# An attention block on one Trainium2 core: one wide transpose and eight small transfers for the softmax maxima

## The chip, the cores and the metric

The kernel is one program on one core of a Trainium2 chip. The metric is the device time of one execution in microseconds (us), the median over the runs.

## What is computed

The input is x (8 batches, 512 tokens, 128 features). Per batch the reference does, in float32:

```python
h = layernorm(x) * (1 + ca) + sa
x = x + ga * attention(h)        # 16 heads of 8 features, rotary, causal, softmax, projection
h = layernorm(x) * (1 + cb) + sb
x = x + gb * spikes(relu(h @ W_fc.T)**2 @ W_proj.T)   # counts of 5 threshold steps / 5
```

What matters for this change is the softmax: the weights are exp(scale * (q.k - m)) over the allowed keys, divided by their sum, and m is the row maximum of the scores of one query and one head.

## The kernel before, in words

**Halves.** The work goes in 16 halves, two per batch; a half is 8 of the 16 heads of one batch. The scores are computed twice. The first time the queries lie on the partitions (`scores_for_max`, L442, into `s_bank`, 21 units a half) and VectorE (DVE) reduces each block to a negated maximum (`maxima`, L771, the reduction at L783, into `negmax`, 128 x 8 x 4: queries of 64 for two heads on the partitions, eight blocks `i` of 64 queries, four pairs of heads `p`). The second time the keys lie on the partitions (`scores_for_exp`, L477, into `t_bank`, 18 units `u` or slots a half), ScalarE (ACT) takes the exponential of a whole unit (L669), and TensorE multiplies it by the values (`probs_times_v`, L505, into `o_bank`).

**How the maximum gets into the second product.** q and k are stored as rows of `qf` and `kf` (72 rows: three bfloat16 parts of q, k for 8 features). Two more rows, `FR:KX`, hold in `qf` the negated maximum in two bfloat16 parts (high and remainder), and ones in `kf`, so that the second product comes out with the maximum already subtracted. Those rows need the maxima laid out as rows along the queries, and `negmax` has them as columns. The way from one to the other, once per half, is:

- GpSimd (POOL) splits `negmax` into two bfloat16 parts `mparts` (`split_maxima`, L1028 and L1030);
- TensorE turns them (`transpose_maxima`, L464): eight transposes of 128 x 8 into `m_bank`, which is the bank `a_bank` read as bfloat16; it gives 8 rows of 1024;
- ACT copies the 8 x 1024 block to `mrow` (`maxima_out`, L675);
- SP sends `mrow` with one transfer to the two rows of `qf` (`place_maxima`, L356) and the semaphore `maxrow` counts its landing;
- the first `scores_for_exp` of the half waits for `maxrow` (L480).

I call the point where TensorE goes from the last slot of half n-1 to the first slot of half n **boundary n** (boundary 0 is the first slot of all).

**What sets the order.** Every engine has its instruction list written out by hand; there is no planner. TensorE's list per slot is: maxima scores up to `scores_ahead(u)` (31 units in advance), then the exp scores of the slot, then products with the values, then, in given slots, the transposes of the maxima (slot `M_AT` = 14 of 18), projections of a later batch (`A_AT`), and projection and feed-forward of an earlier one (`D_AT`, `Y_AT`). ACT copies the maxima just ahead of the exponential of slot 15. The list of TensorE is strictly in order at the level of waits: while the first slot of a half waits for `maxrow`, nothing behind it starts.

**SP's queue.** All transfers go through SP, in a written order (L402 to L425). After `place_maxima(n)` come stores of q and k parts (L333), and `spread` (L345, L351), which loads `qf` and `kf` for the half after next and waits until the exp scores of the half before are all done; then `move_outputs` with four transfers of `den` and four of `o_t` (L362, L366), and `spread_reciprocals`. A `den` transfer goes from 2 partitions of 512 float32 to 16 partitions of 64.

Of the kernel before, what the change touches and what calls it, by code (L numbers as in the profile page):

```python
# [7 lines left out]
BF16 = mybir.dt.bfloat16  # L8
ALU = mybir.AluOpType
# [3 lines left out]
P = 128  # L13
NB, SEQ, D = 8, 512, 128
# [4 lines left out]
FR = NPART * NPART * HD  # L19
MR = 2  # L20
KX = FR + MR
# [7 lines left out]
C = 64  # L29
NC = SEQ // C  # L30
HALVES = 2 * NB
HP = 4
HH = 2 * HP
NP = H // 2
RING = 3
# [76 lines left out]
def reach(eng, sem, count):  # L112

    if count > 0:
        eng.wait_ge(sem, count)


def adaln_kernel(nc, x, wqk, bqk, wv, bv, wo, bo, wfc, wpr, ct, wmod, cosn, sinn, place, out):
# [9 lines left out]
    with ExitStack() as ctx:  # L128
        def sb(name, shape, dt=F32):
            return ctx.enter_context(nc.sbuf_tensor(name, shape, dt))  # L130
# [4 lines left out]
        def sem(name):  # L135
            return ctx.enter_context(nc.semaphore(name))
# [15 lines left out]
        identb = sb("identb", [P, P], BF16)  # L152
# [29 lines left out]
        qf = sb("qf", [P, RING, HH, SEQ], BF16)  # L182
        kf = sb("kf", [P, RING, HH, SEQ], BF16)
        negmax = sb("negmax", [P, 2, NC, HP])
        mparts = sb("mparts", [P, NC, MR, HP], BF16)
        mrow = sb("mrow", [MR * HP, 2 * SEQ], BF16)
        probs = sb("probs", [P, NU, SEQ])
        o_raw = sb("o_raw", [P, 2, SEQ])
        o_t = sb("o_t", [P, SEQ])
# [24 lines left out]
        m_bank = a_bank[:, :].bitcast(BF16)  # L214
# [40 lines left out]
        maxrow = [sem("maxrow0"), sem("maxrow1")]  # L255
        s_ready = sem("s_ready")
        s_free = sem("s_free")
        mhigh_done = sem("mhigh_done")
        mparts_done = sem("mparts_done")
        m_ready = sem("m_ready")  # L260
        m_free = sem("m_free")
# [46 lines left out]
        def _(sp):  # L308
# [43 lines left out]

            def place_maxima(n):
                sp.wait_ge(m_free, n + 1)
                dst = qf[FR:KX, n % RING].rearrange("r (p a) c -> r p (a c)", a=2)
                sp.dma_start(dst, mrow[:, :]).then_inc(maxrow[n % 2], 16)  # L356

            def move_outputs(b, half):
                sp.wait_ge(o_free, 2 * b + half + 1)
# [36 lines left out]
            for j in range(NPART):  # L396
                store_part(1, 0, j)
            place_maxima(0)
            for j in range(NPART - 1):
                store_part(1, 1, j)  # L400

            for b in range(NB):  # L402
                if b + 1 < NB:
                    store_part(b + 1, 1, 2)
                    spread(2 * b + 2)
                if b > 0:
                    move_outputs(b - 1, 1)
                    spread_reciprocals(b - 1, 1)
                if b + 3 < NB:
                    load_x(b + 3)  # L410
                place_maxima(2 * b + 1)
                if b + 1 < NB:
                    spread(2 * b + 3)
                if b > 1:
                    store_out(b - 2)
                move_outputs(b, 0)
                spread_reciprocals(b, 0)
                if b + 2 < NB:
                    for j in range(NPART):
                        store_part(b + 2, 0, j)  # L420
                    store_part(b + 2, 1, 0)
                if b + 1 < NB:
                    place_maxima(2 * b + 2)
                if b + 2 < NB:
                    store_part(b + 2, 1, 1)  # L425
# [8 lines left out]
        def _(pe):  # L434
            def by_halves(bank, cols, weights, data, start=True, stop=True):

                for a in range(2):
                    own = slice(C * a, C * (a + 1))
                    last = nc.tensor.matmul(bank[own, cols], weights[:, own], data, start=start, stop=stop)  # L439
                return last  # L440
# [23 lines left out]
            def transpose_maxima(n):  # L464
                pe.wait_ge(mparts_done, n + 1)
                reach(pe, m_free, n)

                if n % 2 == 0:
                    pe.wait_ge(a_free, 3 * min(n // 2 + 2, NB))
                else:  # L470
                    pe.wait_ge(v_placed, 2 * min((n - 1) // 2 + 2, NB))
                for i in range(NC):
                    to = m_bank[0:MR * HP, :].rearrange("m (a q) -> m a q", a=2)[:, :, C * i:C * (i + 1)]
                    last = nc.tensor.transpose(to, mparts[:, i].rearrange("p r h -> p (r h)"), identb[:, :])
                last.then_inc(m_ready, 1)

            def scores_for_exp(u):  # L477
                n, v = divmod(u, NU)
                if v == 0:
                    pe.wait_ge(maxrow[n % 2], 16 * (n // 2 + 1))  # L480
                reach(pe, e_done, u - 1)
                bank, slot = t_bank[u % 2], n % RING
                blocks = T_BANKS[v]
                for at, (p, kb, col) in enumerate(blocks):
                    w = SEQ - C * kb
                    for a in range(2):
                        nc.tensor.matmul(bank[C * a:C * (a + 1), col:col + w],  # L487
                                         kf[0:KX, slot, 2 * p + a, C * kb:C * (kb + 1)],
                                         qf[0:KX, slot, 2 * p + a, C * kb:SEQ], start=at == 0, stop=False)
                for at, (p, kb, col) in enumerate(blocks):  # L490
                    for a in range(2):
                        last = nc.tensor.matmul(bank[C * a:C * (a + 1), col:col + C], identb[:, C * a:C * (a + 1)],  # L492
                                                causal_t[:, C * a:C * (a + 1)], start=False, stop=at == len(blocks) - 1)
                last.then_inc(t_ready, 1)
# [106 lines left out]
            for k in range(NS, NS + 3):  # L601
                scores_for_max(k)
            transpose_maxima(0)
            for k in range(NS + 3, scores_ahead(-1)):
                scores_for_max(k)
            pe.wait_ge(ones_placed, 16)

            for u in range(SLOTS):
                n, v = divmod(u, NU)
                b, at = divmod(u, PER_BATCH)  # L610
                for k in range(scores_ahead(u - 1), scores_ahead(u)):
                    scores_for_max(k)
                scores_for_exp(u)
                for kb in PV_AFTER.get(v, ()):
                    probs_times_v(n, kb)
                if n > 0:
                    for kb in PV_LATE.get(v, ()):
                        probs_times_v(n - 1, kb)
                if v == M_AT and n + 1 < HALVES:
                    transpose_maxima(n + 1)  # L620
                if at in A_AT and b + 1 < NB:
                    a_task(b + 1, A_AT[at])
                if at - PER_BATCH in A_AT and b + 2 < NB:
                    a_task(b + 2, A_AT[at - PER_BATCH])
                steps, products = (D_LAST, Y_LAST) if b == final else (D_AT, {})
                if at in steps and b > 0:
                    d_task(b - 1, steps[at])
                if at in products:
                    d_task(b - 1, Y_, range(products[at], products[at] + 1))
                if at + PER_BATCH in Y_AT and b > 1:  # L630
                    d_task(b - 2, Y_, range(Y_AT[at + PER_BATCH], Y_AT[at + PER_BATCH] + 1))
# [15 lines left out]
            for t, cols in enumerate(tokens):  # L647
                pe.wait_ge(last_on, t + 1)
                last = by_halves(d_bank, cols, o_n[:, cols], wo_g[:, final % 2, :])
# [5 lines left out]
            for i in range(NF):  # L655
                pe.wait_ge(last_sq, i + 1)
                for t, cols in enumerate(tokens):
                    last = by_halves(d_bank, cols, sq[:, i, cols], wpr_sb[:, i, :], i == 0 and t == 0,
                                     i == NF - 1 and t == NT - 1)
# [3 lines left out]
        def _(act):  # L663
# [7 lines left out]
            def maxima_out(n):  # L671
                act.wait_ge(m_ready, n + 1)
                if n > 0:
                    act.wait_ge(maxrow[(n - 1) % 2], 16 * ((n - 1) // 2 + 1))
                nc.scalar.copy(mrow[:, :], m_bank[0:MR * HP, :]).then_inc(m_free, 1)  # L675

            def modulate1(b):
                act.wait_ge(a_ready, 4 * b + T1 + 1)
# [63 lines left out]
            for u in range(SLOTS):  # L742
                n, v = divmod(u, NU)
# [280 lines left out]
        def _(pool):  # L1024
            def split_maxima(n):
                pool.wait_ge(s_free, NS * (n + 1))
                reach(pool, m_ready, n)
                nc.gpsimd.tensor_copy(mparts[:, :, 0, :], negmax[:, n % 2]).then_inc(mhigh_done, 1)  # L1028
                pool.wait_ge(mhigh_done, n + 1)
                nc.gpsimd.tensor_tensor(mparts[:, :, 1, :], negmax[:, n % 2], mparts[:, :, 0, :],  # L1030
                                        ALU.subtract).then_inc(mparts_done, 1)

            def inverse_deviation(b, mv, ve, rs, var_done, eps_done, done):
                pool.wait_ge(var_done, b + 1)
# [72 lines left out]
            for a in range(2):  # L1107
# [3 lines left out]
                last = nc.gpsimd.affine_select(out=ones, in_=ones, pattern=[[0, 2 * NC * NP], [0, HD]], fill=0.0,  # L1111
                                               compare_op=ALU.is_ge, base=(C - 1, -C)[a],
                                               channel_multiplier=(-1, 1)[a])
# [94 lines left out]
```

## Time and profile before

| what | value |
|---|---|
| runs | 474.01, 469.62, 468.40 us; median 469.62 |
| the profiled execution | 470.54 us, its span 468.8 us |
| granted TensorE clock, mean | 0.921 of full |
| busy share | PE 85%, PEld 53%, DVE 68%, ACT 54%, POOL 26% |
| transfers of `mrow` to `qf` | 16, 16 KB each |

The span is what the trace covers; 1.7 us of the execution lie outside it. PE is TensorE's matmuls, PEld its weight loads, SPq the queue of SP. A busy PE is not PE at its peak, since the ends of matmuls are modelled. The chain of work goes back from the last instruction to what released each step.

### The profile page before, as it was taken

To read this page: it belongs to the slowest core of one execution; us is meant where nothing else is said; L and a number is where in the kernel's file an instruction comes from. 1 tells how busy PE (TensorE), PEld (TensorE's weight loads), DVE (VectorE), ACT (ScalarE), POOL (GpSimd) and SP (SyncE) were. 2 spreads that over 40 slices of the span, in tenths; PEclk is the share of its full clock that TensorE was granted. 3 is DMA by queue.
4 is the path that set the end of the run, shared out by engine and by line. 5 is a ranking of instruction groups with operands and counts; after the bars stand their busy time and mean duration, and the time that the engine had idled before them with its cause. 6 is when DMAs were issued, how large, how long until landed. Compare 5 with 4: busy or idle time off the path is not lost.

```text
span 468.8 us, 15244 instructions
## 1 busy us (share of the span) xinstructions
PE 396.8 (85%) x6423; PEld 248.3 (53%) x6423; DVE 320.3 (68%) x719; ACT 252.5 (54%) x445; POOL 124.1 (26%) x159
## 2 busy tenths in 40 slices
PE   3448999978898999999989999999998899778562
PEld 2213655545545765576557655665575657536322
DVE  2759848856785699759884988499848745530825
ACT  1202246647568556955586567656764666665120
POOL 7615002240324032503250325023511300220210
PEclk9856559989999999999999999999998999999857
DMA  6055622232322424141414151414141410110000
GB/s 206 34 169 149 202 70 60 78 102 79 95 71 71 116 74 110 66 127 47 133 59 129 48 138 59 126 29 137 53 116 48 108 47 6 27 38 13 24 0 23
DMA packets 26046, 38.50 MB, mean 82 GB/s; under 512 B 5794, under 2 KB 20714, under 8 KB 23690
## 3 DMA queue, kind: packets, MB, share of 16 engines
q1 hardware_dynamic: 25978, 37.53, 27.9%
q8 instruction: 50, 0.82, 0.8%
q14 instruction: 18, 0.15, 0.1%
HBM read 26.35 MB, written 8.65 MB: 75 GB/s over the span
## 4 chain that ended last, share of the span: by engine, by line
PE 42%; DVE 18%; DMA 17%; SPq 7%; ACT 7%; issue 5%; POOL 2%; POOLq 0%; ACTq 0%; DVEq 0%
PE o_bank L505 9%; PE d_bank L439 8%; PE s_bank L454 7%; PE t_bank L487 6%; DVE negmax L783 6%; DMA qf<-mrow 5%; SPq L362 4%; DMA den<-o_raw 4%; DMA kf<-k_scr 3%; PE a_bank L439 3%; DVE rot_s L819 3%; DMA rden<-r_scr 2%; DVE count L850 2%; ACT mrow L675 2%; PE a_bank L532 2%
## 5 line engine op out<-in xcount | busy, mean ns | idle before, releaser
L783 DVE TENSOR_REDUCE negmax<-s_bank 128x1 f32<-128x448 f32 (+7 forms) x368 | 193.2, 563 | 72.6 <-PE s_bank L460 70.3
L669 ACT ACTIVATE probs<-t_bank 128x512 f32<-128x512 f32 x288 | 166.1, 595 | 99.2 <-PE t_bank L492 96.4
L454 PE MATMUL s_bank<-kf,qf 72*64 72x448 bf16 (+7 forms) x1024 | 125.3, 311 | 12.5 <-DVE negmax L783 9.3
L487 PE MATMUL t_bank<-qf,kf 74*64 74x512 bf16 (+7 forms) x1024 | 114.5, 294 | 13.0 <-DMA qf<-mrow 7.4
L454 PEld LDWEIGHTS s_bank<-kf,qf 72*64 72x64 bf16 x1024 | 51.3, 115 | 57.5 <-DVE negmax L783 33.6
L505 PE MATMUL o_bank<-probs,v 128*32 128x512 f32 (+7 forms) x1024 | 78.6, 427 | 0.0
L460 PE MATMUL s_bank<-causal,identb 128*64 128x64 bf16 x1024 | 75.2, 201 | 0.0
L492 PE MATMUL t_bank<-causal_t,identb 128*64 128x64 bf16 x1024 | 65.1, 195 | 0.0
L487 PEld LDWEIGHTS t_bank<-qf,kf 74*64 74x64 bf16 x1024 | 41.9, 112 | 34.2 <-DMA qf<-mrow 11.6
L460 PEld LDWEIGHTS s_bank<-causal,identb 128*64 128x64 bf16 x1024 | 49.7, 117 | 8.4 <-issue 8.2
L492 PEld LDWEIGHTS t_bank<-causal_t,identb 128*64 128x64 bf16 x1024 | 48.3, 112 | 10.2 <-issue 0.8
L505 PEld LDWEIGHTS o_bank<-probs,v 128*32 128x32 f32 x1024 | 27.4, 112 | 38.8 <-issue 27.7
L1028 POOL CAST mparts<-negmax 128x32 bf16<-128x32 f32 x16 | 3.4, 210 | 127.5 <-DVE negmax L783 127.5
L1050 POOL TENSOR_TENSOR whole<-rot_c,rot_s 128x512 f32<-128x512 f32 x15 | 19.0, 1268 | 63.1 <-DVE rot_s L819 63.0
L439 PE MATMUL d_bank<-wpr_sb,sq 128*64 128x128 f32 x512 | 33.8, 276 | 1.1 <-ACT sq L712 1.1
L439 PE MATMUL d_bank<-h2T,wfc_sb 128*64 128x512 f32 x112 | 29.9, 613 | 1.7 <-ACT relu L707 1.2
L439 PEld LDWEIGHTS d_bank<-wpr_sb,sq 128*64 128x64 f32 x512 | 27.6, 137 | 6.2 <-issue 5.0
L707 ACT ACTIVATE relu<-d_bank 128x512 f32<-128x512 f32 x28 | 16.5, 589 | 16.8 <-PE d_bank L439 16.8
L1060 POOL TENSOR_TENSOR parts<-rest,parts 128x512 bf16<-128x512 f32 x15 | 17.5, 1166 | 22.4 <-ACT parts L718 22.4
L819 DVE SCALAR_TENSOR_TENSOR rot_s<-a_bank,bqk_sb,sin_sb 64x512 f32<-64x512 f32 x30 | 22.5, 750 | 1.0
L439 PE MATMUL a_bank<-hT,wqk_sb 128*64 128x512 f32 x60 | 18.7, 705 | 3.3 <-ACT hT L679 1.9
L690 ACT COPY v<-a_bank 64x512 f32<-64x512 f32 x16 | 9.3, 579 | 20.4 <-PE o_bank L505 19.1
(102 smaller groups left out, 385.3 us busy)
## 6 DMA issues: line engine op xcount, KB each, us to landing
qf<-q_scr SPq DMA_DIRECT2D x15, 576.0 KB
kf<-k_scr SPq DMA_DIRECT2D x45, 192.0 KB
q_scr<-parts SPq DMA_DIRECT2D x24, 128.0 KB, 1.7
k_scr<-parts SPq DMA_DIRECT2D x24, 128.0 KB, 1.7
xa<-in_x SPq DMA_DIRECT2D x8, 256.0 KB, 4.0
o_t<-o_raw SPq DMA_DIRECT2D x60, 32.0 KB, 2.3
rden<-r_scr SPq DMA_DIRECT2D x15, 128.0 KB
out_y<-count SPq DMA_DIRECT2D x7, 256.0 KB, 7.4
```

Of the source, the lines that this page charges most:

```text
L362: sp.dma_start(den[16 * j:16 * (j + 1), half, :], o_raw[32 * j + 16:32 * j + 32:HD, half, :])\
L439: last = nc.tensor.matmul(bank[own, cols], weights[:, own], data, start=start, stop=stop)
L454: nc.tensor.matmul(bank[C * a:C * (a + 1), col:col + keys], qf[0:FR, slot, 2 * p + a, C * i:C * (i + 1)], kf[0:FR, slot, 2 * p + a, 0:keys ...
L460: last = nc.tensor.matmul(bank[C * a:C * (a + 1), end - C:end], identb[:, C * a:C * (a + 1)], causal[:, C * a:C * (a + 1)], start=False, s ...
L487: nc.tensor.matmul(bank[C * a:C * (a + 1), col:col + w], kf[0:KX, slot, 2 * p + a, C * kb:C * (kb + 1)], qf[0:KX, slot, 2 * p + a, C * kb: ...
L492: last = nc.tensor.matmul(bank[C * a:C * (a + 1), col:col + C], identb[:, C * a:C * (a + 1)], causal_t[:, C * a:C * (a + 1)], start=False, ...
L505: last = nc.tensor.matmul(o_bank[32 * p:32 * (p + 1), C * kb:SEQ], v32[:, b % 2, NP * kb + HP * half + p, :], probs[:, v, col:col + w], st ...
L669: nc.scalar.activation(probs[:, v, :], t_bank[u % 2][:, :], ACT.Exp, scale=SCALE).then_inc(e_done, 1)
L783: last = nc.vector.tensor_reduce(own[:, i, p:p + len(same)], cols, AX.X, ALU.max, negate=True)
L819: nc.vector.scalar_tensor_tensor(dst[to, qk, :], bank[of, :], bqk_sb[of, qk:qk + 1], table[of, :], ALU.add, ALU.mult).then_inc(rotated if ...
L1050: nc.gpsimd.tensor_tensor(whole[:, qk, :], rot_c[:, qk, :], rot_s[:, qk, :], ALU.add)\
L1060: nc.gpsimd.tensor_tensor(parts[:, qk, 2, :], rest[:, qk, :], parts[:, qk, 1, :], ALU.subtract).then_inc(split_done, 1)
```

## The change

`mparts` is laid out with the pair of heads outermost, then the part, then the block of 64 queries, so that its 64 columns can be turned at once. One transpose of 128 x 64 gives 64 rows of 128. ACT's copy to `mrow` takes 64 x 128 in place of 8 x 1024. Row 16 p + 8 r + i of `mrow` holds, for pair p, part r and block i, two runs of 64 queries, one for each head of the pair. SP sends eight transfers, one per head, each from 16 partitions of 64 elements to the head's two rows of `qf`. The semaphore's counts are multiplied by eight. `split_maxima` reads `negmax` in the other order of its two free dimensions.

```diff
--- before.py
+++ after.py
@@ -182,8 +182,8 @@
         qf = sb("qf", [P, RING, HH, SEQ], BF16)
         kf = sb("kf", [P, RING, HH, SEQ], BF16)
         negmax = sb("negmax", [P, 2, NC, HP])
-        mparts = sb("mparts", [P, NC, MR, HP], BF16)
-        mrow = sb("mrow", [MR * HP, 2 * SEQ], BF16)
+        mparts = sb("mparts", [P, HP, MR, NC], BF16)
+        mrow = sb("mrow", [MR * HP * NC, P], BF16)
         probs = sb("probs", [P, NU, SEQ])
         o_raw = sb("o_raw", [P, 2, SEQ])
         o_t = sb("o_t", [P, SEQ])
@@ -352,8 +352,10 @@
 
             def place_maxima(n):
                 sp.wait_ge(m_free, n + 1)
-                dst = qf[FR:KX, n % RING].rearrange("r (p a) c -> r p (a c)", a=2)
-                sp.dma_start(dst, mrow[:, :]).then_inc(maxrow[n % 2], 16)
+                for p in range(HP):
+                    for a in range(2):
+                        src = mrow[MR * NC * p:MR * NC * (p + 1), C * a:C * (a + 1)]
+                        sp.dma_start(qf[FR:KX, n % RING, 2 * p + a], src).then_inc(maxrow[n % 2], 16)
 
             def move_outputs(b, half):
                 sp.wait_ge(o_free, 2 * b + half + 1)
@@ -469,15 +471,13 @@
                     pe.wait_ge(a_free, 3 * min(n // 2 + 2, NB))
                 else:
                     pe.wait_ge(v_placed, 2 * min((n - 1) // 2 + 2, NB))
-                for i in range(NC):
-                    to = m_bank[0:MR * HP, :].rearrange("m (a q) -> m a q", a=2)[:, :, C * i:C * (i + 1)]
-                    last = nc.tensor.transpose(to, mparts[:, i].rearrange("p r h -> p (r h)"), identb[:, :])
-                last.then_inc(m_ready, 1)
+                nc.tensor.transpose(m_bank[0:MR * NC * HP, 0:P], mparts[:, :, :, :].rearrange("p h r i -> p (h r i)"),
+                                    identb[:, :]).then_inc(m_ready, 1)
 
             def scores_for_exp(u):
                 n, v = divmod(u, NU)
                 if v == 0:
-                    pe.wait_ge(maxrow[n % 2], 16 * (n // 2 + 1))
+                    pe.wait_ge(maxrow[n % 2], 16 * HH * (n // 2 + 1))
                 reach(pe, e_done, u - 1)
                 bank, slot = t_bank[u % 2], n % RING
                 blocks = T_BANKS[v]
@@ -671,8 +671,8 @@
             def maxima_out(n):
                 act.wait_ge(m_ready, n + 1)
                 if n > 0:
-                    act.wait_ge(maxrow[(n - 1) % 2], 16 * ((n - 1) // 2 + 1))
-                nc.scalar.copy(mrow[:, :], m_bank[0:MR * HP, :]).then_inc(m_free, 1)
+                    act.wait_ge(maxrow[(n - 1) % 2], 16 * HH * ((n - 1) // 2 + 1))
+                nc.scalar.copy(mrow[:, :], m_bank[0:MR * NC * HP, 0:P]).then_inc(m_free, 1)
 
             def modulate1(b):
                 act.wait_ge(a_ready, 4 * b + T1 + 1)
@@ -1025,10 +1025,11 @@
             def split_maxima(n):
                 pool.wait_ge(s_free, NS * (n + 1))
                 reach(pool, m_ready, n)
-                nc.gpsimd.tensor_copy(mparts[:, :, 0, :], negmax[:, n % 2]).then_inc(mhigh_done, 1)
+                own = negmax[:, n % 2].rearrange("p i h -> p h i")
+                nc.gpsimd.tensor_copy(mparts[:, :, 0], own).then_inc(mhigh_done, 1)
                 pool.wait_ge(mhigh_done, n + 1)
-                nc.gpsimd.tensor_tensor(mparts[:, :, 1, :], negmax[:, n % 2], mparts[:, :, 0, :],
-                                        ALU.subtract).then_inc(mparts_done, 1)
+                nc.gpsimd.tensor_tensor(mparts[:, :, 1], own, mparts[:, :, 0], ALU.subtract)\
+                    .then_inc(mparts_done, 1)
 
             def inverse_deviation(b, mv, ve, rs, var_done, eps_done, done):
                 pool.wait_ge(var_done, b + 1)
```

## Rows read from the trace of the kernel before

**Rows 1.** the page, part 1 and the clock's line of part 2 (forty slices)

```profile
PE 396.8 (85%) x6423; PEld 248.3 (53%) x6423; DVE 320.3 (68%) x719; ACT 252.5 (54%) x445; POOL 124.1 (26%) x159
...
PEclk9856559989999999999999999999998999999857
```

**Rows 2.** the page, part 4: the chain that ended last, by engine and line

```profile
PE o_bank L505 9%; PE d_bank L439 8%; PE s_bank L454 7%; PE t_bank L487 6%; DVE negmax L783 6%; DMA qf<-mrow 5%; SPq L362 4%; DMA den<-o_raw 4%; DMA kf<-k_scr 3%; PE a_bank L439 3%; DVE rot_s L819 3%; DMA rden<-r_scr 2%; DVE count L850 2%; ACT mrow L675 2%; PE a_bank L532 2%
```

**Rows 3.** tile `mrow`: ns min/median/max, starts; then who waited, us, times

```profile
L675 ACT COPY mrow<-a_bank x16: 984/996/1002, 50.7 to 407.0; 8x1024 bf16<-8x1024 bf16 x16
L356 SPq DMA_DIRECT2D qf<-mrow x16: 672/695/707, 51.8 to 408.0; - x16
...
  PEld t_bank L487: 11.6, 13
```

**Rows 4.** timeline at boundary 6: start us, us, work, [idle before <-releaser]

```profile
192.93 0.61 PE L474 MATMUL a_bank<-identb,mparts 128*8 128x128 bf16 x8
...
194.34 1.00 ACT L675 COPY mrow<-a_bank 8x1024 bf16<-8x1024 bf16 x1
...
197.68 0.41 PE L487 MATMUL t_bank<-qf,kf 74*64 74x512 bf16 x2 [0.82 <-DMA qf<-mrow]
```

**Rows 5.** chain in order of time: start us, us, what (transfers until landed)

```profile
146.90 3.09 DMA qf<-mrow
...
195.37 2.27 DMA qf<-mrow
198.12 1.00 PE o_bank L505 x16
199.12 1.08 PE a_bank L532 x32
...
255.64 2.21 DMA den<-o_raw
```

**Rows 6.** timeline of SP alone: start us, us issuing, transfers

```profile
213.92 0.39 SPq L325 DMA_DIRECT2D xa<-in_x  x1
...
225.76 2.69 SPq L362 DMA_DIRECT2D den<-o_raw  x4
```

**Rows 7.** line L729, a copy of 128 columns out of PSUM

```profile
L729 ACT COPY gate_t<-d_bank x1: 254/254/254, 32.1 to 32.1; 24x128 f32<-24x128 f32 x1
```

**Rows 8.** timeline at boundary 7, columns as rows 4

```profile
217.55 0.60 ACT L669 ACTIVATE probs<-t_bank 128x512 f32<-128x512 f32 x1 [0.97 <-PE t_bank L492]
...
218.04 0.98 ACT L675 COPY mrow<-a_bank 8x1024 bf16<-8x1024 bf16 x1
...
222.72 1.80 DVE L783 TENSOR_REDUCE negmax<-s_bank 128x1 f32<-128x512 f32 x3
```

**Rows 9.** timeline at boundary 0 and at boundary 15, columns as rows 4

```profile
50.74 1.00 ACT L675 COPY mrow<-a_bank 8x1024 bf16<-8x1024 bf16 x1 [5.54 <-PE a_bank L474]
...
55.01 0.18 PEld L487 LDWEIGHTS t_bank<-qf,kf 74*64 74x64 bf16 x2 [0.25 <-issue]
...
408.01 0.70 SPq L356 DMA_DIRECT2D qf<-mrow  x1
...
412.31 0.11 PEld L487 LDWEIGHTS t_bank<-qf,kf 74*64 74x64 bf16 x2 [0.30 <-ACT probs L669]
```

**Rows 10.** timeline at boundary 3, columns as rows 4

```profile
120.20 0.69 SPq L356 DMA_DIRECT2D qf<-mrow  x1
...
122.16 1.09 PE L439 MATMUL d_bank<-wo_g,o_n 128*64 128x128 f32 x16 [1.89 <-POOL o_n L1082]
```

**Rows 11.** stretches at boundary 2: us, PE busy (x), PEclk, DMA share, GB/s

```profile
98.00:100.00 2.00, 0.75 (x16) 1.00 0.19 66
...
102.00:104.00 2.00, 2.00 (x24) 0.50 0.50 123
```

**Rows 12.** chain behind boundary 2, columns as rows 5

```profile
101.76 1.86 PE o_bank L505 x16
103.62 1.50 PE a_bank L532 x32
```

## The prediction

> **What bounds the kernel now.** I read the page first. TensorE is busy 85% of the span and its clock is full except at the start and at a few places [rows 1]. The chain that ended last runs over TensorE most of the time, but two pieces of the way of the maxima stand on it by name: the transfer of `mrow` with 5% and ACT's copy to `mrow` with 2% [rows 2]. The chain says where this comes from: at a boundary of halves it leaves TensorE, goes through the copy and through the transfer up to its landing, and comes back to the first exp scores. So I went by the tile `mrow`: 16 copies of 0.996 us, 16 transfers of which SP issues each in 0.695 us, and 13 times TensorE's weight load waited for the landing, 11.6 us in all [rows 3]. At boundary 6 the eight transposes take 0.61 us from 192.93, the copy starts at 194.34 and takes 1.00, and TensorE resumes at 197.68 [rows 4]; from the start of the issue to the landing it is 2.27 us [rows 5]. The boundary is therefore set by this chain at 13 of 16 places: anything added to it is added to the time, unless something behind gives it back.
>
> **The change, step by step.**
>
> *Transposes.* One in place of eight saves about 7/8 of 0.61 us, 0.53 us of TensorE per half [rows 4]. I cost it at nothing. TensorE comes to the boundary earlier and waits longer. The copy does not start earlier either: at boundary 7 it starts 0.49 us after the exponential before it started (217.55, 218.04) [rows 8], so ACT's own order holds it, not the transposes. If that cover were gone, the gain would be 15 x 0.53 = 8 us.
>
> *The copy.* 8 x 1024 becomes 64 x 128; time goes by the columns. The nearest row is a copy of 128 float32 columns in 0.254 us [rows 7]. Taken as 0.27, the chain gets shorter by 0.72 us.
>
> *The transfers.* Eight issues in place of one, on one queue. No row shows this form, but `den` is its mirror: 2 partitions to 16, pieces of 256 bytes, where the new one goes from 16 partitions to 2 in pieces of 128 bytes. Four `den` transfers keep SP for 2.69 us, 0.66 from one start to the next [rows 6]. The short end is the 0.39 us of another transfer [rows 6], the long end the 0.70 of today's `mrow` [rows 3]. I take 0.66, the mirror. The eighth transfer starts 7 x 0.66 = 4.62 us after the first (2.7 to 4.9 at the ends).
>
> *The landing.* From the last issue's start I take 2.27 us, as now; the fourth of a `den` group landed after 2.21 although three had gone just before [rows 5], so small transfers one behind another do not pile up. The long end is 3.09, which one `mrow` transfer took [rows 5].
>
> *Sum for the chain of one boundary:* 4.62 - 0.72 = 3.9 us later (2.0 at the short issue, 5.0 with long issues and the long landing in a few).
>
> *The queue behind it.* Stores of q and k parts and the loads of `spread` stand behind `place_maxima` and start later by 4 us. I cost this at nothing: SP is free again at the end of the last issue, 2.27 - 0.66 = 1.6 us before TensorE resumes, just as now, so relative to TensorE nothing is late. POOL's split reads `negmax` in another order, 128 x 32 elements, and POOL waits for DVE anyway: nothing.
>
> *Boundaries.* Thirteen pay in full: 13 x 3.9 = 50.7. Three have room. Boundary 15: landed at 408.01 + 2.27 = 410.3, resumed at 412.31 [rows 9], room 2.0, pays 1.9. Boundary 3: landed at 120.20 + 2.27 = 122.5; a projection that had waited for POOL runs from 122.16 to 123.3 [rows 10] and the last slot behind it to about 124.0, room 1.5, pays 2.4. Boundary 0: copy at 50.74, so landed at 54.0, first scores at 55.01 [rows 9], room 1.0; here the transposes are on the chain (ACT had waited 5.54 us for them) and their saving, 0.9 us at the half clock, counts, so it pays 2.0. Together 57.0 us.
>
> *Given back.* DVE works off a backlog across the odd boundaries: behind boundary 7 it is still at reductions from 222.72 for 1.80 us [rows 8], and TensorE then waits for it. A longer stop lets DVE finish. I give 1 us for each of five such boundaries: -5.
>
> *The clock.* Each stop of TensorE becomes 0.8 + 3.9 = 4.7 us with no matmul in it. At boundary 2 TensorE was busy 0.75 of 2.00 us, in two gaps, and right behind it the granted clock stood at 0.50, the lower of its two levels (1.2 GHz) [rows 11]; the products with the values took 1.86 us there against 1.00 at boundary 6, the next block 1.50 against 1.08 [rows 5, 12]: with the first scores (0.64 against 0.41) 1.5 us lost. A stop of 4.7 us is more than twice those gaps, so I expect the fall at nearly every one of the 13, and a longer stretch at the lower level. Bounds: nothing, to 3.4 us (all 3.4 us of dense work behind an even boundary taking double). I take 1.8, a little over boundary 2, where the stop was shorter: 13 x 1.8 = +23. The Trainium skill (TensorE: Matmul & The Clock Gate, HAM oscillation) has the same pattern as a rule: a loop in which every round waits long for a transfer falls to the lower clock in every round. By that rule the 23 us are there; by boundaries 4 to 12, where the clock stayed full through stops of about 1 us [rows 1, 4], they would not be, and the sum would be 52.
>
> *Sum:* 57 - 5 + 23 = 75 us on the profiled execution of 470.5, 545.5 us. The median of the runs is 0.9 lower, so I say 545.
>
> **Rivals.**
>
> 1. *The clock costs nothing* (it stays full, or the work behind a boundary was waiting anyway): 470 + 52 = 522, from 512 to 533. For: stops of 1 us left it full, and ACT and DVE have room. Against: rows 11. Chance 0.22.
> 2. *The issues are cheaper*, near the 0.39 us of the short transfer: 7 x 0.42 - 0.72 = 2.2 us a boundary, 30 us in all with the room taken off, and with some clock 500 to 512. Against: the mirror transfer takes 0.66. Chance 0.10.
> 3. *The clock stays low for long* after each stop, since work that waits on DVE and ACT does not raise it: in this kernel it stood at its half level through slices 4 and 5, while the first half's slots ran [rows 1, 9]. Then over 3.4 us a boundary, above 571. Chance 0.05.
> 4. *The chain gets shorter* and the kernel is not slower: the copy gives 0.72 us, and this decides if an additional transfer costs SP under 0.72 / 7 = 0.10 us. Then, at an issue of 0.05, the boundary comes 0.37 us earlier, 15 x 0.37 = 5.5 us, 464 us. The Trainium skill (DMA: Bandwidth & Descriptors, Anatomy of one DMA) has a rule of this kind, for GpSimd's path: about 50 ns of dispatch, descriptor generation small, most of a transfer's fixed cost in its completion, which overlaps. The trace speaks against: SP's issues follow one another at 0.66 us. That nothing is seen because TensorE had room is excluded by 13 waits [rows 3]. Chance 0.03.
>
> **How the numbers follow.** The likeliest case has 0.60 and runs by itself from 533 to 571. The range takes in case 1 whole on its lower side: 513 to 568; out of it stay cases 2, 3 and 4 and the edge of the main one, nearly 0.2. A measurement of this kernel can tell about 2% from no change. All cases but the fourth are slower by more; it is 1.2% faster, so it goes to "same" for the most part. Slower 0.96, same 0.02, faster 0.02.
>
> **What would show it.** SP's `mrow` issues: 128 of them, 0.62 to 0.70 us each, eight in about 5.3 us; the copies at 0.25 to 0.30 us; TensorE's transposes 16 instead of 128; TensorE's waits for `mrow` at about 11.6 + 57 = 69 us in all; the clock's line with falls at most boundaries, the mean below 0.85. The prediction fails if the issues overlap, if the last landing takes much longer than 2.3 us because eight transfers share few engines, or if the clock stays full.

## The result: 17.6% slower, and the profile after

| | runs, us | median | profiled execution | its span | clock |
|---|---|---|---|---|---|
| before | 474.01, 469.62, 468.40, 469.35 | 469.49 | 470.54 | 468.8 | 0.921 |
| after | 551.24, 546.92, 552.22, 557.74 | 551.73 | 551.24 | 549.5 | 0.870 |

The ratio is 1.176, with a 95% interval of 1.168 to 1.183. The forecast was 545 us, range 513 to 568. Here and below, a ratio and its interval leave out a kernel's executions that lie over 1.5% above its fastest one, while the medians are over all of them.

The page of the changed kernel first: part 1, the clock's line of part 2, and the lines of part 4 (it answers to [rows 1, 2]).

```profile
PE 428.9 (78%) x6311; PEld 261.6 (48%) x6311; DVE 321.8 (59%) x719; ACT 243.5 (44%) x445; POOL 124.4 (23%) x159
...
PEclk9999995967787986979897989798989998968957
...
SPq L358 13%; PE o_bank L505 13%; PE d_bank L441 10%; PE t_bank L487 9%; PE s_bank L456 9%; DMA qf<-mrow 5%; DVE negmax L783 4%; PE a_bank L441 3%; DVE count L850 3%; PE a_bank L532 2%; PE t_bank L492 2%; PE s_bank L462 2%; DVE rot_s L819 1%; DMA kf<-k_scr 1%; POOL whole L1051 1%
```

TensorE's instructions are 112 fewer, yet it is busy 32 us longer (428.9 against 396.8), and the rest of the span, in which it is idle, grew by 49 us (120.6 against 72.0). 32 and 49 make the 81 us by which the span grew. So there are two losses, not one: time in which TensorE stands, and time in which it does the same work more slowly (in the kernel before 52 of its busy us fell into stretches at the lower clock, in the changed one 111). On the chain SP's issues of the maxima (L358), which were not among the lines of [rows 2], now have 13%, and the clock's line has dips all along where it was full before.

The tile `mrow` (columns as in [rows 3]); the last line is that of the kernel before:

```profile
L358 SPq DMA_DIRECT2D qf<-mrow x128: 610/611/723, 50.4 to 487.6; - x128
L675 ACT COPY mrow<-a_bank x16: 246/248/259, 50.1 to 482.6; 64x128 bf16<-64x128 bf16 x16
...
  PEld t_bank L487: 69.8, 16
  PE t_bank L487: 65.0, 16
```

```profile
  PE t_bank L487: 7.4, 10
```

There are 128 issues of 0.61 us in place of 16 of 0.695, a copy of 0.248 us in place of 0.996, and TensorE waits at all 16 boundaries: its weight loads 69.8 us in place of 11.6 (13 times), its matmuls, the other side of the same wait, 65.0 us in place of 7.4 (10 times).

The chain at boundary 7, in order of time, in the kernel before [rows 8] and in the changed one:

```profile
218.04 0.99 ACT mrow L675
...
219.05 2.27 DMA qf<-mrow
...
221.37 0.41 PE t_bank L487 x2
```

```profile
257.10 0.26 ACT mrow L675
257.37 0.69 SPq L358
...
258.10 0.61 SPq L358
...
262.02 1.66 DMA qf<-mrow
...
263.73 0.64 PE t_bank L487 x2
```

The copy starts at 257.10 and TensorE resumes at 263.73: 6.63 us, against 3.33 before. The eight issues follow one another every 0.665 us on the mean (4.65 us from the first start to the eighth), and the eighth has landed 1.66 us after its own start. Over all 16 boundaries the way from the copy's start to TensorE's first exp scores grew by 50 us in sum: by 3.3 at most odd boundaries, by 3.5 at most even ones.

And what lies behind a boundary, here boundary 8 (windows of the granted clock: stretch, us, PE busy and count, clock, DMA share, GB/s; then the chain):

```profile
287.00:289.00 2.00, 0.62 (x14) 1.00 0.11 33
289.00:291.00 2.00, 0.00 (x0) 0.99 0.02 4
291.00:293.00 2.00, 0.29 (x2) 0.50 0.20 67
...
295.00:297.00 2.00, 2.00 (x38) 0.50 0.82 229
```

```profile
292.71 0.64 PE t_bank L487 x2
...
293.40 1.86 PE o_bank L505 x16
295.26 1.91 PE a_bank L532 x32
297.17 1.23 PE d_bank L441 x16
```

TensorE stops for 5.09 us, the clock goes to its lower level (0.50, 1.2 GHz) inside the stop, and the first work behind it takes 0.64, 1.86, 1.91 and 1.23 us, where [rows 4, 5] have 0.41, 1.00 and 1.08 (the fourth took 0.88 at boundary 6). That is 2.3 us lost at this boundary, beside the longer stop. In the 3 us behind each of boundaries 1 to 15 the mean granted clock was 0.50 to 0.68.

### The profile page after: what moved, and what is told of

The parts are those of the page before. It is cut to its first block, busy times and chain, and to the rows that moved or that the text cites. A ratio compares the mean times of both kernels' runs of the same rounds, so it can differ in the third digit from the quotient of the medians.

```text
span 549.5 us, 15132 instructions
## 1 busy us (share of the span) xinstructions
PE 428.9 (78%) x6311; PEld 261.6 (48%) x6311; DVE 321.8 (59%) x719; ACT 243.5 (44%) x445; POOL 124.4 (23%) x159
## 4 chain that ended last, share of the span: by engine, by line
PE 53%; DVE 14%; SPq 14%; DMA 7%; issue 4%; ACT 4%; POOL 3%; POOLq 0%; ACTq 0%; DVEq 0%
SPq L358 13%; PE o_bank L505 13%; PE d_bank L441 10%; PE t_bank L487 9%; PE s_bank L456 9%; DMA qf<-mrow 5%; DVE negmax L783 4%; PE a_bank L441 3%; DVE count L850 3%; PE a_bank L532 2%; PE t_bank L492 2%; PE s_bank L462 2%; DVE rot_s L819 1%; DMA kf<-k_scr 1%; POOL whole L1051 1%
## 5 line engine op out<-in xcount | busy, mean ns | idle before, releaser
L487 PE MATMUL t_bank<-qf,kf 74*64 74x512 bf16 (+7 forms) x1024 | 126.1, 316 | 70.3 <-DMA qf<-mrow 65.0
L456 PE MATMUL s_bank<-kf,qf 72*64 72x448 bf16 (+7 forms) x1024 | 132.3, 325 | 9.4 <-DVE negmax L783 8.3
L505 PE MATMUL o_bank<-probs,v 128*32 128x512 f32 (+7 forms) x1024 | 92.3, 488 | 0.0
L487 PEld LDWEIGHTS t_bank<-qf,kf 74*64 74x64 bf16 x1024 | 45.4, 118 | 95.9 <-DMA qf<-mrow 69.8
L456 PEld LDWEIGHTS s_bank<-kf,qf 72*64 72x64 bf16 x1024 | 55.4, 120 | 57.0 <-DVE negmax L783 29.7
L462 PE MATMUL s_bank<-causal,identb 128*64 128x64 bf16 x1024 | 79.2, 207 | 0.0
L492 PE MATMUL t_bank<-causal_t,identb 128*64 128x64 bf16 x1024 | 69.0, 202 | 0.0
L492 PEld LDWEIGHTS t_bank<-causal_t,identb 128*64 128x64 bf16 x1024 | 52.1, 118 | 11.6 <-issue 3.5
L462 PEld LDWEIGHTS s_bank<-causal,identb 128*64 128x64 bf16 x1024 | 53.3, 122 | 8.8 <-issue 8.2
L505 PEld LDWEIGHTS o_bank<-probs,v 128*32 128x32 f32 x1024 | 29.9, 123 | 47.5 <-issue 38.6
```

The costliest lines, as they stand in the source:

```text
L456: nc.tensor.matmul(bank[C * a:C * (a + 1), col:col + keys], qf[0:FR, slot, 2 * p + a, C * i:C * (i + 1)], kf[0:FR, slot, 2 * p + a, 0:keys ...
L462: last = nc.tensor.matmul(bank[C * a:C * (a + 1), end - C:end], identb[:, C * a:C * (a + 1)], causal[:, C * a:C * (a + 1)], start=False, s ...
L487: nc.tensor.matmul(bank[C * a:C * (a + 1), col:col + w], kf[0:KX, slot, 2 * p + a, C * kb:C * (kb + 1)], qf[0:KX, slot, 2 * p + a, C * kb: ...
L505: last = nc.tensor.matmul(o_bank[32 * p:32 * (p + 1), C * kb:SEQ], v32[:, b % 2, NP * kb + HP * half + p, :], probs[:, v, col:col + w], st ...
```

## The experiments

Two theories at the start. **Queue and clock:** SP issues eight transfers one after another, which sets back each boundary, and the longer stop takes the clock down. **Rivals:** A, the small pieces or their landing cost the time, not the number of transfers; B, the wide transpose, the copy or POOL's reordered split have a part in it; C, the lower clock lies beside waits and costs nothing; D, transfers wait for one another in the DMA engines, so it matters little who issues them.

### e1: the kernel before, its one transfer cut into eight

```diff
-                dst = qf[FR:KX, n % RING].rearrange("r (p a) c -> r p (a c)", a=2)
-                sp.dma_start(dst, mrow[:, :]).then_inc(maxrow[n % 2], 16)
+                for p in range(HP):
+                    for a in range(2):
+                        src = mrow[p:MR * HP:HP, SEQ * a:SEQ * (a + 1)]
+                        sp.dma_start(qf[FR:KX, n % RING, 2 * p + a], src).then_inc(maxrow[n % 2], 16)
```

> The kernel before with its eight narrow transposes and its 8 x 1024 copy, but with the 16 KB sent in eight transfers, one per head (two pieces of 1 KB each). Theory (SP issues eight transfers one after another, and the longer stop takes the clock down): the copy stays at 1.00 us, so the boundary comes 0.75 us later still than in the changed kernel, 551 + 13 x 0.75 = about 561 us; TensorE's waits for mrow about 75 us in all. Rival A (the small pieces of 128 bytes or the landing of mrow from 64 rows are the cost, not the number of transfers): with pieces of 1 KB most of the loss goes, under 500 us. Rival B (the wide transpose, the copy or POOL's reordered split cost part of it): under 545 us.

Measured: 568.62, 571.43, 572.23 and 545.05 us. The tile and one landing on the chain:

```profile
L358 SPq DMA_DIRECT2D qf<-mrow x128: 562/563/657, 51.8 to 504.8; - x128
...
  PE t_bank L489: 57.5, 16
```

```profile
172.39 1.59 DMA qf<-mrow
...
174.71 1.86 PE o_bank L507 x16
```

Eight transfers alone, with everything else as before, cost all of the loss (the changed kernel took 547 to 558). Rivals A and B fall: pieces of 1 KB help nothing, and there is no wide transpose here. Of the expected figures the time was near (561), but not for the reason given. I had added 0.75 us a boundary for the slower copy; from the copy's start to the exp scores it was 6.9 to 7.0 us, only 0.1 to 0.3 more than in the changed kernel, since the issues came every 0.61 us. The waits were 57.5 us and not 75, for that reason and because TensorE still does eight transposes, 10.2 us in all against 3.6, and so comes to its wait later. What made the profiled execution longer is the clock: behind boundaries 7, 9 and 11 it stood at its lower level for 16 us, and each of these halves took 33.1 us, where the changed kernel's trace has 5 us and 29.0. Among the four executions three with a mean clock of 0.827 to 0.833 took 569 to 572 us, the one with 0.893 took 545. The mean alone does not order the times, though: the changed kernel took 546.92 us at 0.850 and 551.24 at 0.870.

### e2: the changed kernel, the stop filled with matmuls

```diff
                 if v == 0:
+                    if 0 < n < HALVES - 1:
+                        pe.wait_ge(m_free, n + 1)
+                        for _ in range(FILL):
+                            nc.tensor.matmul(a_bank..., identb[:, :], causal...,
+                                             start=True, stop=True)
                     pe.wait_ge(maxrow[n % 2], 16 * HH * (n // 2 + 1))
```

`FILL` is 14.

> The changed kernel, and at each boundary but the first and the last TensorE does 14 matmuls of 512 bfloat16 columns into the idle a_bank (their result is used by nothing) behind the copy of the maxima and ahead of the wait for mrow: about 3.0 us of work inside a stop of 3.4 to 5.1 us. Theory (a part of the loss, 23 us predicted, is the lower clock behind each stop): the granted clock stays full at the boundaries, mean above 0.93, the products with the values behind a boundary take 1.00 and not 1.87 us, and the time falls by 20 to 28 us to 524 to 532. Rival C (the lower clock lies beside waits and costs nothing): the clock is full but the time stays within 5 us of 551. If the filler itself were in the way, the time would rise.

Measured: 525.29 us median, ratio to before 1.122 (1.112 to 1.132), so 26 us less than the changed kernel by the medians (25 by the ratios, and their intervals leave some 6 us either way) although TensorE has 196 more matmuls to do. The clock at boundary 6 and the work behind it:

```profile
221.00:223.00 2.00, 2.00 (x11) 1.00 0.02 3
223.00:225.00 2.00, 0.52 (x3) 1.00 0.02 3
225.00:227.00 2.00, 1.48 (x23) 1.00 0.38 132
```

```profile
225.96 1.00 PE o_bank L511 x16
```

The maxima land as late as in the changed kernel, but the clock is full through the stop and the products with the values take 1.00 us. Rival C falls: about 26 us of the loss went with the clock. At some boundaries it still fell (boundary 2 had 1.87 us for the same block), and the mean clock was 0.898 in the profiled execution and 0.903 to 0.945 in the others, mostly under the expected 0.93, so the clock's whole share is likely to be more than that.

### e3: the eight transfers issued by two engines

```diff
-                for p in range(HP):
+                for p in range(HP // 2):
...
                 nc.scalar.copy(mrow[:, :], m_bank[0:MR * NC * HP, 0:P]).then_inc(m_free, 1)
+                act.wait_ge(m_free, n + 1)
+                for p in range(HP // 2, HP):
+                    for a in range(2):
+                        src = mrow[MR * NC * p:MR * NC * (p + 1), C * a:C * (a + 1)]
+                        act.dma_start(qf[FR:KX, n % RING, 2 * p + a], src).then_inc(maxrow[n % 2], 16)
```

> The changed kernel with its eight transfers issued by two engines: SP issues the four of the first two pairs of heads, ACT the four others right behind its copy. Theory (the serial issue on one queue is the cost): the two issue side by side, the last landing comes 4 x 0.665 = 2.66 us earlier, TensorE's waits fall from 65 to about 28 us, and with part of the clock given back the time is 495 to 516 us. Rival D (the transfers wait for each other in the DMA engines, two engines for all of them, or in the shared making of descriptors): the last landing stays where it was and the time stays near 551 us. ACT is kept from its exponentials of slots 15 to 17 for 2.6 us, which costs up to 1 us a half if it decides.

Measured: 512.94 us, ratio 1.097 (1.088 to 1.106). The timeline at one boundary (start, us, engine, work), and TensorE's wait for ACT:

```profile
348.65 3.10 SPq L358 DMA_DIRECT2D qf<-mrow  x4
348.66 2.67 ACTq L680 DMA_DIRECT2D qf<-mrow  x4
...
351.44 1.82 ACT L669 ACTIVATE probs<-t_bank 128x512 f32<-128x512 f32 x3 [2.81 <-issue]
```

```profile
PE t_bank L487 <- ACT probs L669: 38.2, 31, 3.8
```

SP's four and ACT's four run side by side, in 3.10 and 2.67 us in place of 5.26. Rival D falls in its strong form; there is a small part of it: SP's issues come every 0.78 us instead of 0.665. TensorE hardly waits for `mrow` (7.6 us), but now for ACT, 38.2 us (5.2 in the changed kernel), since ACT's exponentials of the last slots stand behind its own issues; I had priced that at up to 1 us a half and it was twice that. Issue time is a cost wherever it is put.

### e4 to e7: eight, four, two, one

For fewer transfers the maxima must lie in the order of the destination row. Pairing head p with head p + 4 of the half, rather than 2p with 2p + 1, makes that possible. The core of the edit, with two transfers:

```diff
+                for r in range(MR):
+                    for a in range(2):
+                        own, to = slice(C * a, C * (a + 1)), C * r + HP * NC * a
+                        last = nc.tensor.transpose(m_bank[to:to + HP * NC, 0:C], mparts[own, r]..., identb[own, own])
...
+                nc.scalar.copy(mrow[:, :], m_bank[:, 0:C]).then_inc(m_free, 1)
...
+                for r in range(MR):
+                    dst = qf[FR + r:FR + r + 1, n % RING].rearrange("r h (i c) -> r (h i) c", c=C)
+                    sp.dma_start(dst, mrow[C * r:C * (r + 1), :]).then_inc(maxrow[n % 2], 16)
```

e4 cuts each `r` into four transfers, e5 into two, e7 sends both `r` in one. The 16 KB and the 128 pieces of 128 bytes are the same in all four.

> Control for the three runs beside it. The two heads of a pair are now 4 heads apart (pair p holds heads p and p + 4 of the half), so that the maxima of one part of the split (high or remainder) lie in mrow as 64 rows of 64 in the order of the destination row; four transposes of 64 x 32 make it, and the copy is 128 x 64. The first half's q and k need twice as many transfers at the start. Eight transfers carry the maxima (16 rows to one row each). Theory: SP's eight issues again, copy 0.2 us, so as the changed kernel, plus up to 3 us at the start: 548 to 556 us, one landing 1.65 us behind the last issue's start.

> As the control, but four transfers in place of eight, with the same 128 pieces of 128 bytes in all. Theory (number of issues, plus the clock): against the kernel before, a boundary comes at -0.8 (copy) + 3 x 0.66 (issues) - 0.6 (landing) = +0.6 us; the stop is 1.4 us, the clock mostly stays full; 468.5 + 15 x 0.6 + 3 = about 480 us (474 to 490). Rival A (the small pieces are the cost): nothing changes against the control, near 550.

> As the control, but two transfers, one for each part of the split, 64 rows of 128 bytes into one row of 8 KB. Theory: a boundary comes at -0.8 + 0.66 - 0.6 = -0.7 us against the kernel before; 468.5 - 13 x 0.7 + 3 = 462 us (455 to 468), faster than both kernels if the start costs no more than 3 us. Rival A: near 550. Rival E (more pieces in one transfer make it land later, as they share few DMA engines): the landing is later than 1.65 us by what the pieces cost and the time is 468 or more.

> As the control, but one transfer of all 128 rows of 128 bytes to the two rows. Theory: no second issue, so 0.66 us less than with two, if the landing stays at 1.65 to 2.3 us: 450 to 462 us. Rival E: both destination rows are one piece list on two DMA engines, 64 pieces each, and the landing goes to 3 us or more; then 465 to 480 us.

| transfers | median, us | ratio to before (interval) | TensorE waits for `mrow`, us (matmul side) |
|---|---|---|---|
| 8 (e4) | 558.55 | 1.185 (1.171 to 1.199) | 64.9 |
| 4 (e5) | 495.11 | 1.046 (1.033 to 1.058) | 29.7 |
| 2 (e6) | 470.41 | 0.999 (0.993 to 1.004) | 10.3 |
| 1 (e7) | 469.73 | 1.006 (1.000 to 1.011) | 6.3 |

The kernel before had a median of 471.34 us beside them, over 19 runs. e6 had one execution of 1920 us among its ten; I have no cause for it, and the median does not hang on it.

From 8 to 4 each transfer less gives 15.9 us, from 4 to 2 12.3 us, from 2 to 1 0.7 us. 16 boundaries of 0.63 us would be 10 us; I put the rest of the first two steps down to the clock and, in e5, to late landings, without a run that parts them, and the last step is worth nothing. That follows the queue-and-clock theory down to two transfers, and refutes A again, since the pieces stayed the same. Rival E stays open: one transfer with all 128 pieces landed 2.14 to 2.60 us after its start, one with 64 pieces mostly 1.84, one with 16 mostly 1.70, but the bytes grow with the pieces here, and the 16 KB of the kernel before, in eight pieces, took 2.27.

All four sums were too low. e4 came out just above its 548 to 556. e5 was 15 us above the 480 that I expected: at ten boundaries the last transfer landed after 1.70 to 1.76 us, as priced, but at six after 2.5 to 4.1, and the clock, which I had left nearly full, was at 0.871 in the profiled execution. For e6 and e7 I expected 462 and 450 to 462.

### e8 to e10: why a shorter way of the maxima gains nothing

The chain of e7 at boundary 6 gives a reason:

```profile
198.35 1.23 POOL whole L1057
...
199.66 0.63 ACT parts L724
...
200.31 0.32 SPq L333
...
200.68 2.30 DMA qf<-mrow
...
203.02 0.41 PE t_bank L493 x2
```

The copy is not on it. What is there is POOL's sum for the rotary embedding of a batch two further on, ACT's cast of it, and SP's store of that cast, which stand ahead of the copy and of the transfer on ACT and on SP. e8 takes e7 and changes both orders, e9 does the same to the kernel before, e10 is e8 with fewer transfers at the start.

```diff
-            TAKE_AT = {-8: (0, 0), -6: (0, 1), -4: (1, 0), -2: (1, 1)}
+            TAKE_AT = {-8: (0, 0), -6: (0, 1), -3: (1, 0), -2: (1, 1)}
...
-                    store_part(b + 2, 1, 0)
                 if b + 1 < NB:
                     place_maxima(2 * b + 2)
                 if b + 2 < NB:
+                    store_part(b + 2, 1, 0)
                     store_part(b + 2, 1, 1)
```

> The one-transfer kernel, and two instructions change places at the boundaries of two batches: ACT's cast of the first k part comes behind its copy of the maxima (slot -3 in place of -4), and SP's store of that part behind the transfer of the maxima. In the one-transfer run the copy stood right behind that cast, which had waited for POOL, and SP's transfer right behind its store. Theory F (that is why the shorter way of the maxima gained nothing at every second boundary): the copy starts up to 1 us earlier at 6 boundaries, and the time falls by 3 to 7 us against the one-transfer kernel, to 463 to 467 us. Rival G (the start, with eight transfers more for q and k of the first half, and DVE decide): no change, 469 to 471.

> The kernel before with the same two places changed. Theory F: the copy is freed from the cast here too; up to 3 us less than before (465 to 469 of 470). Rival G: no change. If it gains as much as the run beside it, then the order alone is the gain and the one wide block with one transfer is worth nothing here.

> As the first of these three, but q and k of the first half are loaded in four transfers for all eight heads in place of sixteen for two groups of four heads; TensorE's first scores wait for all of them. Rival G (the start is what took the gain away): SP is free about 8 us earlier, but the first scores start later by the landing of twice the bytes; 2 to 4 us less than the run beside it. Theory F alone: within 2 us of it.

Measured: e8 470.08 us, ratio 1.003 (0.999 to 1.008); e9 470.31, 1.000 (0.995 to 1.006); e10 466.80, 0.988 (0.979 to 0.998), with the kernel before at 472.12 beside them. Timeline and tile of e8:

```profile
191.84 0.21 ACT L681 COPY mrow<-a_bank 128x64 bf16<-128x64 bf16 x1
...
193.07 0.61 ACT L724 CAST parts<-whole 128x512 bf16<-128x512 f32 x1
```

```profile
  PE t_bank L493: 0.8, 2
```

The edit did what it was meant to: the copy (191.84) now comes ahead of the cast (193.07), and TensorE waits 0.8 us for `mrow` in the whole execution. The time did not move, where Theory F had 463 to 467. So Theory F described a real order, but not the bound. e8's boundaries say where the gain went. TensorE reaches boundary 2 at 97.7 (101.1 before), boundary 8 at 243.6 (246.2), and boundary 9 at 271.4 (269.6): 3.4 and 2.6 us ahead, then 1.8 behind. The chain of that one half, and the clock in it:

```profile
240.60 0.18 ACT mrow L681
...
241.94 0.52 ACT parts L724
...
242.52 1.16 POOL rest L1063
...
244.46 1.18 POOL parts L1067
...
245.65 2.63 DMA k_scr<-parts
...
249.71 8.55 DMA kf<-k_scr
...
258.30 0.64 PE s_bank L458 x2
```

```profile
255.00:259.00 4.00, 1.12 (x24) 0.68 0.23 64
259.00:263.00 4.00, 4.00 (x32) 0.50 0.03 8
```

The maxima scores of the half after next need `kf`. POOL's last split of k ends at 245.64, then come the store (2.63 us), the loads (8.55 us), and only at 258.30 the scores. TensorE stood 2.9 us for `kf` here, longer than any single wait for `mrow` in the kernel before (1.6), and the clock fell behind it.

That split is not independent of the edit. The chain goes back from it, over POOL's remainder (242.52), to ACT's cast of the first k part (241.94), which the edit has moved behind the copy of the maxima (240.60). At boundary 8 POOL's last split of k ended 1.4 us after TensorE had resumed in the kernel before and 0.8 in e7, but 2.1 in e8 and in e9, the two with the new order. TensorE's waits for `kf` over the whole execution, in the kernel before, e9, e7 and e8 (us in total, times, longest):

```profile
PE s_bank L454 <- DMA kf<-k_scr: 1.0, 2, 0.7
```

```profile
PE s_bank L454 <- DMA kf<-k_scr: 5.0, 7, 1.2
```

```profile
PE s_bank L458 <- DMA kf<-k_scr: 5.7, 5, 2.5
```

```profile
PE s_bank L458 <- DMA kf<-k_scr: 14.6, 11, 2.9
```

The new order took 5.5 us off the waits for `mrow` from e7 to e8 (6.3 to 0.8) and put 8.9 on those for `kf`; from the kernel before to e9 it took off 3.9 (7.4 to 3.5) and put on 4.0. So the edit handed the wait from one transfer to the other. Why e6 and e7 gained nothing is less clear: their waits for `kf` grew by 1.8 and 4.7 us, but e7 waits for `mrow` almost as long as the kernel before (6.3 us), behind the cast. No run shortened the way to `kf`. For rival G speak e8 and e9, which stayed where it had them, and e10, 3.3 us under e8 where it had 2 to 4. e10 alone lies below the kernel before, by 1.2%, but that ratio rests on three executions and its interval ends just under 1.

## Why the prediction was right, point by point

**The transposes: right.** They were cut from 128 to 16, 10.4 us of TensorE in all to 3.6, and TensorE waited that much longer, as the prediction says.

**The copy: right.** 0.248 us against the 0.27 taken.

**The issues: right.** 0.665 us from start to start, against 0.66 from the mirror transfer `den` [rows 6]. e5 and e3 show that this term decides: with four issues on SP's queue in place of eight, three quarters of the loss went in e5, and nearly half in e3, where ACT paid for the other four.

**The landing: mis-sized.** I took 2.27 us as in [rows 5]; it was 1.64 to 1.68: the new transfers carry 2 KB and landed sooner than the one of 16 KB. The `den` row's 2.21 us, with other transfers right behind it, I read as a confirmation of 2.27; it was none. So a boundary came 3.3 us later (3.5 at the even ones) and not 3.9: 43 us over the thirteen full boundaries in place of 51. The three with room paid 2.3, 1.6 and 2.7 us, together about what I gave them. The chain's sum was 50 and not 57.

**The queue behind: right.** At boundary 7 SP ends the last issue at 262.63 and starts the loads of `spread` at 262.73, a microsecond before TensorE resumes; it waited 0.3 us in the whole execution for `kf` ahead of maxima scores.

**Waits in all: the number right, by luck.** The weight loads waited 69.8 us where I had 69. But I had added only the chain's 57 to what there was; the chain gave 50, and the shorter transposes, which the prediction names as a longer wait but leaves out of this sum, about 7 more.

**Given back: the size about right, the place not.** I gave 5 us. TensorE's idle time grew by 49 us where its waits for `mrow` grew by 58, so 9 us of idle time went elsewhere. Its waits for DVE's maxima, where I had expected it, fell only from 9.3 to 8.3 us.

**The clock: the mechanism right, the size too small.** I took 1.8 us at each of thirteen boundaries, 23 us. e2 shows about 26 and does not take the clock's falls away everywhere, and TensorE's busy time grew by 32 us in spite of fewer instructions. I had also taken one stop of 4.7 us for all thirteen; from boundary 4 to 12 it was 5.1 us at the even ones and 3.4 to 3.5 at the odd ones, and the clock fell at both. What my 1.8 us lacked is a piece of rival 3, which I had held at 0.05: after some stops the clock did not come back with the next dense work. Windows of the changed kernel behind boundary 5:

```profile
204.00:206.00 2.00, 2.00 (x20) 0.50 0.83 249
...
212.00:214.00 2.00, 2.00 (x26) 0.50 0.09 21
...
216.00:218.00 2.00, 2.00 (x48) 1.00 0.04 8
```

TensorE is busy by the record in all of them, and the clock is at its lower level for about 12 us. That half took 33.0 us against 24.7 before (8.3 longer), and the second half, with the same stretch, 30.9 against 22.9. The halves from the seventh to the twelfth were each 4.1 to 5.3 us longer, which is the 3.3 to 3.5 of the chain and 1 to 2 for the clock. The Trainium skill (TensorE: Matmul & The Clock Gate, HAM oscillation) describes a loop that falls to the lower clock in each round because of its wait for a transfer. The trace agrees: the lower level came behind 15 of the 16 boundaries.

**The rule of rival 4.** The Trainium skill (DMA: Bandwidth & Descriptors, Anatomy of one DMA) gives a small cost of dispatch and descriptors, for GpSimd's path. It does not hold for SP's queue here: each further transfer put the next one 0.65 to 0.73 us later.

So the chain's term was 7 us too large (57 against 50), and clock and giving back together 13 us too small (18 against the 31 us that are left of the 81). The two errors work against each other, and the total of 545 against 552 owes part of its closeness to that.

## What to carry over

Count the transfers on a chain that an engine waits for, not the bytes: each one took the issuing queue 0.6 to 0.8 us here, on SP as on ACT, and the price is read from a transfer of like shape in the trace. Stops that went from mostly under 1 us to between 3.4 and 5.1 us cost more than their length here, because the work behind them ran at the lower clock; price that from a place where it already happens, and allow for stretches in which the clock does not come back at once. And a wait that shows in every round need not be worth its sum: with 7.4 us of it cut to 0.8 in e8 the time stayed where it was, and the waits for `kf` went from 1.0 to 14.6 us. When you move an instruction out of one chain's way, look at whose chain it was on.

## What the runs showed of the hardware

- One program can land in different patterns of the clock: e1 took 545 us at a mean of 0.893 and 569 to 572 at 0.83. In the changed kernel the four means, 0.821 to 0.870, do not order the four times.
- The clock can stay at its lower level for about 12 us while the record has TensorE busy throughout (the changed kernel, 204 to 216 us).
- Two queues, SP and ACT, issue side by side, at 0.78 and 0.67 us a transfer in place of SP's 0.665 alone (e3).
- Sixteen pieces of 128 bytes (2 KB) landed 1.65 us after the start of the issue, 64 pieces (8 KB) mostly after 1.84, 128 pieces (16 KB) after 2.14 to 2.60, and the 16 KB in eight pieces of the kernel before mostly after 2.27.
